# A PSUM bank for VectorE's small operands in a four-layer graph network

## What is computed

```
L0: (1 + eps) * x + segment_sum(relu(x[src] + edge48), dst)
L1: h = in_deg > 0 ? segment_sum(x[src] * ci[src], dst) * cj : x;   relu(h @ W.T + b)
L2: relu(segment_sum(norm * x[col], row) @ W.T + b)
L3: msg = (silu(edge40 @ W1.T + b1) @ W2.T + b2 + logit(type)) * x[dst] * cutoff * node_vec[dst]
    layernorm(x + segment_sum(msg, src) / segment_sum(node_vec[dst], src)) * gamma + beta
```

## Time and profile before

| | us |
|---|---|
| median of 3 runs (3310.13 to 3343.74) | 3333.56 |
| the profiled execution | 3348.9 |
| its span | 3347.1 |
| VectorE busy | 2025.7 (61%) |
| GpSimd busy | 1965.7 (59%) |
| TensorE busy | 774.6 (23%) |
| ScalarE busy | 640.9 (19%) |

### The profile page before, as it was taken

The page is one execution under the profiler, slowest core; times in us unless marked ns, Lnnn a source line. Parts: engine busy times, 40 slices in busy tenths (PEclk is TensorE's granted clock), DMA queues, the critical chain, the costliest instruction groups (busy, mean ns, idle before and its releaser), DMA issues.

```text
span 3347.1 us, 18878 instructions
## 1 busy us (share of the span) xinstructions
PE 774.6 (23%) x3478; PEld 547.8 (16%) x3478; DVE 2025.7 (61%) x2590; ACT 640.9 (19%) x1034; POOL 1965.7 (59%) x1768
## 2 busy tenths in 40 slices
PE   1182000000455653777832200000340000000000
PEld 0020000000355642444522200000340000000000
DVE  2187689768555554444543640788548968948551
ACT  0000102210222222333311100222111223221110
POOL 5703647770355456555247772777757777673776
PEclk7585555555565665555555555555555555555555
DMA  3105827660132232111000299344222212210000
GB/s 107 21 0 199 307 57 282 236 208 11 54 111 95 98 103 55 23 23 23 17 12 16 24 78 78 110 132 133 78 61 66 82 55 78 65 51 6 15 15 15
DMA packets 154317, 268.03 MB, mean 80 GB/s; under 512 B 87656, under 2 KB 112314, under 8 KB 154146
## 3 DMA queue, kind: packets, MB, share of 16 engines
q1 hardware_dynamic: 92786, 198.90, 21.4%
q0 software_dynamic: 56448, 44.04, 7.5%
q10 hardware_dynamic: 5040, 24.69, 2.0%
HBM read 135.62 MB, written 137.21 MB: 82 GB/s over the span
## 4 chain that ended last, share of the span: by engine, by line
issue 23%; POOL 21%; DVE 20%; PE 13%; another core or an unknown queue 9%; ACT 6%; DMA 4%; SPq 1%; DVEq 1%; ACTq 0%; POOLq 0%
POOL ring L425 10%; POOL out L463 6%; POOL x_table L463 5%; ACT sq L568 2%; DVE mu L1261 2%; DVE var L1270 2%; PE psT L845 2%; PE psO L860 2%; DVE du L1264 2%; PE psA L898 2%; PE psA L951 2%; DMA x_table<-sumb,put 1%; PE psG L956 1%; DVE sumb L1207 1%
## 5 line engine op out<-in xcount | busy, mean ns | idle before, releaser
L463 POOL DMA_INDIRECT y_table<-sumb,put x196 | 208.3, 1063 | 309.8 <-ACT sumb L595 252.2
L425 POOL DMA_INDIRECT ring<-in_xaux,srcI x196 | 189.1, 965 | 228.6 <-ACTq L562 141.5
L463 POOL DMA_INDIRECT x_table<-sumb,put x196 | 225.2, 1149 | 158.3 <-ACT sumb L595 91.6
L425 POOL DMA_INDIRECT ring<-edge_records,dstI x196 | 231.6, 1182 | 118.9 <-issue 61.0
L425 POOL DMA_INDIRECT ring<-y_table,srcI x196 | 203.9, 1040 | 159.2 <-ACTq L545 99.5
L425 POOL DMA_INDIRECT ring<-h_by_src,zd x196 | 235.3, 1200 | 89.0 <-issue 60.7
L425 POOL DMA_INDIRECT ring<-x_table,srcI x196 | 228.0, 1163 | 97.9 <-issue 57.9
L425 POOL DMA_INDIRECT ring<-xa_table,dstI x196 | 224.1, 1143 | 103.2 <-issue 64.8
L463 POOL DMA_INDIRECT out<-sumb,put x196 | 220.1, 1123 | 107.7 <-issue 60.8
L831 PE MATMUL psG<-ident,tail 128*49 128x128 f32 x10 | 4.5, 447 | 1137.1 <-DVEq L1013 1093.8
L1270 DVE TENSOR_REDUCE var<-sq 128x28 f32<-128x1344 f32 x119 | 181.2, 1552 | 142.1 <-ACT sq L568 137.1
(11 more groups left out here) (281 smaller groups left out, 3043.0 us busy)
## 6 DMA issues: line engine op xcount, KB each, us to landing
din<-in_xaux SPq DMA_DIRECT2D x56, 728.0 KB
x_table<-do SPq DMA_DIRECT2D x56, 672.0 KB
din<-x_table SPq DMA_DIRECT2D x56, 672.0 KB
xa_table<-din SPq DMA_DIRECT2D x28, 728.0 KB
y_table<-GX SPq DMA_DIRECT2D x28, 672.0 KB
out<-do SPq DMA_DIRECT2D x28, 672.0 KB
records_by_src<-ring ACTq DMA_DIRECT2D x14, 693.0 KB
GX<-records_by_src ACTq DMA_DIRECT2D x14, 693.0 KB
```

The source lines that it names most:

```text
L425: pool.indirect_dma_start(ring[:, h, t, 0:w], None, table, bass.IndirectOffsetOnAxis(ap=of[:, c * H + t:c * H + t + 1], axis=0), **skip).t ...
L463: pool.indirect_dma_start(table, bass.IndirectOffsetOnAxis(ap=put[:, c * H + t:c * H + t + 1], axis=0), stage[:, h, t, :], None, bounds_ch ...
```

## The change

One PSUM bank, `psS`, takes over the place of five small SBUF tiles: the row sums `mu` and the inverse deviations `srs` (28 columns for each of two blocks), the centred bias `rbc`, and copies of gamma (`gammaP`), beta (`betaP`), the carry (`carryP`) and of what `t0` holds at its last step (`t0P`). VectorE writes them there and reads them from there as one of the two tensors of an instruction; the large tensor of the instruction stays in SBUF. The rotating banks of the product go from six to five: `psO1` is gone, and the sixth, seventh and eighth group of a pair use the banks of the first three. The one product of the edge network that used `psO1` uses `psS`, at a time when it holds nothing that is read later.

```diff
-        mu = sb("mu", [P, 2, R])
-        srs = sb("srs", [P, 2, R])
-        rbc = sb("rbc", [P, D])
...
-        psO = [ps("psO0"), ps("psO1"), psA, psB, psC, psG]
+        psS = ps("psS")
+        psO = [ps("psO0"), psA, psB, psC, psG]
+        mu = psS[:, 0:2 * R].rearrange("p (h c) -> p h c", h=2)
+        srs = psS[:, 56:56 + 2 * R].rearrange("p (h c) -> p h c", h=2)
+        rbc, gammaP, betaP, carryP = (psS[:, 112 + k * D:112 + (k + 1) * D] for k in range(4))
+        t0P = psS[:, 304:304 + CE]
...
-                    elif k >= 6:
-                        pe.wait_ge(mm_used.sem, used - 4)
+                    elif k >= 5:
+                        pe.wait_ge(mm_used.sem, used - 3)
...
-                        last = T.matmul(psO[k % 6][:, j * 96:(j + 1) * 96], hT[0:97, g % 2, j * P:(j + 1) * P],
+                        last = T.matmul(psO[k % 5][:, j * 96:(j + 1) * 96], hT[0:97, g % 2, j * P:(j + 1) * P],
...
                 one(V.tensor_copy(carry[:, :], psG[:, P:P + D + 1]))
+                one(V.tensor_copy(carryP, carry[:, 0:D]))
...
-                one(V.tensor_tensor(su[:, :, :], along(mask[:, cols]), down(carry[:, 0:D]), ALU.mult))
+                one(V.tensor_tensor(su[:, :, :], along(mask[:, cols]), down(carryP), ALU.mult))
...
-            one(V.reciprocal(t0[:, :], t0[:, :]))
+            one(V.reciprocal(t0P, t0[:, :]))
...
-                one(V.tensor_tensor(su[:, :, :], M[:, cols, :], along(t0[:, cols]), ALU.mult))
+                one(V.tensor_tensor(su[:, :, :], M[:, cols, :], along(t0P[:, cols]), ALU.mult))
...
             counts(t0[:, :])
+            one(V.tensor_reduce(carry[:, 0:1], rows[:, 0, :], X, ALU.add))
+            one(V.scalar_tensor_tensor(rbc, carry[:, 0:1].broadcast_to([P, D]), -1.0 / D, rows[:, 0, :],
+                                       ALU.mult, ALU.add))
+            V.tensor_copy(gammaP, rows[:, 1, :]).then_inc(own.sem, own.add())
+            one(V.tensor_copy(betaP, rows[:, 2, :]))
             dve.sem_inc(S["by_src"], 1)
...
-                    V.tensor_tensor(DU[h], wide(h, D), down(rbc[:, :]), ALU.add).then_inc(S["centered"], 1)
+                    V.tensor_tensor(DU[h], wide(h, D), down(rbc), ALU.add).then_inc(S["centered"], 1)
...
-                    V.tensor_tensor(DO[h], along(sr2[:, h, :]), down(rows[:, 1, :]), ALU.mult
+                    V.tensor_tensor(DO[h], along(sr2[:, h, :]), down(gammaP), ALU.mult
...
-                    V.tensor_tensor(DU[h], DU[h], down(rows[:, 2, :]), ALU.add).then_inc(own.sem, own.add())
+                    V.tensor_tensor(DU[h], DU[h], down(betaP), ALU.add).then_inc(own.sem, own.add())
```

More of the change, by code:

```diff
@@ L939, in factors @@
                 for g in range(R // 4):
-                    bank = (psB, psC, psB, psC, psB, psC, psO[1])[g]
+                    bank = (psB, psC, psB, psC, psB, psC, psS)[g]
                     pe.wait_ge(ma.sem, ma.up())
@@ L1024, in _ @@
             one(V.tensor_scalar(rows[:, 0, :], rows[:, 0, :], 0.0, None, ALU.max))
-            one(V.tensor_reduce(mu[:, 0, 0:1], rows[:, 0, :], X, ALU.add))
-            one(V.scalar_tensor_tensor(rbc[:, :], mu[:, 0, 0:1].broadcast_to([P, D]), -1.0 / D, rows[:, 0, :],
-                                       ALU.mult, ALU.add))
             dve.sem_inc(S["init"], 1)
@@ L1319, in _ @@
                 norm([(0, su[:, :, :], su[:, :, :], XS[:, cols, :])])
-                one(V.tensor_tensor(M[:, cols, :], XS[:, cols, :], along(t0[:, cols]), ALU.mult))
+                one(V.tensor_tensor(M[:, cols, :], XS[:, cols, :], along(t0P[:, cols]), ALU.mult))
                 dve.sem_inc(S["rows_new"], 1)
@@ L1328, in taken @@
                     V.scalar_tensor_tensor(DU[h][:, 8 * g:8 * g + n, :],
-                                           psO[(4 * h + g) % 6][:, 0:n * D].rearrange("p (c d) -> p c d", d=D), 0.0,
+                                           psO[(4 * h + g) % 5][:, 0:n * D].rearrange("p (c d) -> p c d", d=D), 0.0,
                                            x(g, n), ALU.max, ALU.add).then_inc(mm_used.sem, mm_used.add())
@@ L1375, in factors @@
                     dve.wait_ge(mo.sem, mo.up())
-                    one(V.tensor_tensor(prod, (psB, psC, psB, psC, psB, psC, psO[1])[g][:, 0:4 * Z].rearrange(
+                    one(V.tensor_tensor(prod, (psB, psC, psB, psC, psB, psC, psS)[g][:, 0:4 * Z].rearrange(
                         "p (c z) -> p c z", z=Z), ohd[:, OH[g], :, :], ALU.mult))
@@ L1572, in _ @@
                 carried(cols)
-                one(V.tensor_tensor(su[:, :, :], M[:, cols, :], along(t0[:, cols]), ALU.mult))
+                one(V.tensor_tensor(su[:, :, :], M[:, cols, :], along(t0P[:, cols]), ALU.mult))
                 one(V.tensor_tensor(su[:, :, :], su[:, :, :], XS[:, cols, :], ALU.add))
                 norm([(0, su[:, :, :], su[:, :, :], su[:, :, :])])
-                one(V.tensor_tensor(su[:, :, :], su[:, :, :], down(rows[:, 1, :]), ALU.mult))
-                one(V.tensor_tensor(su[:, :, :], su[:, :, :], down(rows[:, 2, :]), ALU.add))
+                one(V.tensor_tensor(su[:, :, :], su[:, :, :], down(gammaP), ALU.mult))
+                one(V.tensor_tensor(su[:, :, :], su[:, :, :], down(betaP), ALU.add))
                 one(V.tensor_tensor(su[:, :, :], su[:, :, :], XS[:, cols, :], ALU.add))
```

## The result

The changed kernel took **3399.99 us** (median of 4 runs, 3390.99 to 3412.56) beside 3338.65 us of the kernel before: ratio 1.019, 95% interval 1.014 to 1.025. It is 61 us slower where 56 us less were forecast. The profiled execution has a span of 3402.3 us, 55.2 more than before.

A forecast was written before the change was run, and what follows sets the result against it. GpSimd's indirect DMAs, held up by VectorE instructions reading two SBUF tensors, were taken to bound most stages, with `y_table` a chain of other engines. Terms -20 - 5 - 15 - 4 - 14 + 1 + 1 = -56 us gave 3277 us, range 3250 to 3315.

The forecast's parts named there:

- the line on `y_table`: `y_table` stage, 869 to 1264 us: a chain of VectorE, TensorE and ScalarE; GpSimd's stalls go but nobody waited: 0.
- `xa_table`, -20 forecast: `xa_table` stage, bound by GpSimd: its stall over twelve turns falls from 35 to 15 us: -20 us (-16 to -24).
- `edge_records`, -15 forecast: `edge_records` loop: the bound passes to VectorE, which saves six ring waits of about 2.5 us each: -15 us.
- `x_table` gathered and `h_by_src`, -4: Gathers of `x_table` and `h_by_src`, 2361 to 3011 us: VectorE sets the pace, gains only at the ends: -4 us.
- `out`, -14: `out` loop at the program's end: every stall of GpSimd counts, 30.2 us falls to 15: -14 us (-9 to -20).
- `x_table` scatter, -5: `x_table` scatter: less GpSimd stall in its first seven turns, later savings lost waiting for stores: -5 us (-2 to -9).
- Banks, PSUM operands, copies, +2: Added costs: five banks in the dense product +1 us, PSUM operands of VectorE 0, four `carry` copies +1 us.
- Rival (c): Each norm's two short links: readers wait for small PSUM writes just made; at 0.5 us a link 3377 us; 6%.
- (B): Theory after the result: TensorE's signals come late while GpSimd issues indirect DMAs; GpSimd no longer held by VectorE worsens it.
- (C): Theory after the result: VectorE's own PSUM reads and writes disturb TensorE, at most together with GpSimd's issues.

The follow-up runs named there:

- free chip: Chip where VectorE gets 196 or 197 instructions done at 50 to 100 us beside GpSimd's DMAs; changed kernel against the kernel before: 0.982 to 0.983.
- second job: Changed kernel run once more as it is, against the kernel before, on another chip: ratio 0.982, 2901.6 us against 2955.4.
- paced kernel before: Kernel before with one short GpSimd memset, and a wait for it, ahead of each indirect DMA of the `y_table` and `x_table` scatters: 1.027 of the kernel before.
- third job's two kernels: Against the kernel before: the changed kernel, 0.983; and six banks with SBUF operands in the product loops, PSUM operands elsewhere, 0.987.
- coupled chips: Chips where VectorE gets only 18 to 20 instructions done at 50 to 100 us beside GpSimd's DMAs; changed kernel against the kernel before: 1.018 and 1.019.

## Why the prediction was wrong

**The failed step** is the line on `y_table`: "the stage is a chain between VectorE, TensorE and ScalarE. Stalls go, nobody waited for them. **0**." The chain is right and so is it that nobody waited for GpSimd. Missing is that on this chip the chain runs at a speed that depends on what GpSimd does. On the chip of the result the 0 was +24 us in the scatter and +34 in the gather behind it, in whose second turn the last pair of the product stands; the same omission made `x_table` +34 instead of -5 and the stretch from the first gather of `x_table` to the first of `h_by_src` (2414.9 to 2758.4 us, before 2361.0 to 2688.8), which holds the w2 product, +16 instead of about -2.

The trace of before had the sign. In the earlier trace rows TensorE and VectorE are each busy little more than half of the time and ScalarE a quarter; I read that as dependence alone. The two windows shown above, with VectorE at 5.93 of 50 us beside 41 issues and at 50 of 50 where GpSimd rests, lie in a stretch where the change has no term, and I read nothing there.

**The other terms.** A free chip shows them without the disturbance. No trace of the kernel before as it is was taken on one, so I set the changed kernel of the second job beside the paced kernel before; they differ in the two scatters in more than the change but not in the other tables:

- `xa_table`, -20 forecast: first to last start 283.3 us against 303.1, **-19.8**. On the chip of the result it was 299.1 against 324.0.
- `edge_records`, -15 forecast: start to the start of the next gather 284.4 against 292.7, **-8.3**. Six waits for the ring of 2.49 us went, as said, but each gave way to another:

```profile
2291.54 1.29 DVE L1493 TENSOR_TENSOR sub<-ring 128x672 f32<-128x672 f32 x1
2295.23 1.66 DVE L1206 TENSOR_TENSOR_SCAN sumb<-mask,sub 128x720 f32<-128x720 bf16 x1 [2.40 <-ACT mask L534]
2296.80 2.99 DVE L1462 TENSOR_TENSOR du<-din,psS 128x1344 f32<-128x1344 f32 x2
```

(Timeline of the changed kernel, the place of the earlier trace rows.) The scan waits 2.40 us for ScalarE's copy of the mask, where before it waited 0.85: that copy had been made while VectorE stood at the ring. Of 2.49 us 1.55 are handed on, and an iteration takes 41.7 us instead of 42.7. What was next late behind the ring I had not looked up.

- `x_table` gathered and `h_by_src`, -4: -1.6 us.
- `out`, -14: 267.7 us against 280.1, **-12.4**.
- `x_table` scatter, -5: 6.0 us between the third job's two kernels, which differ in the operands of these loops.
- Banks, PSUM operands, copies, +2: nothing against it in any run.

Together with 3 us in `y_table` that is some 51 us of 56. The total on free chips was -54, -49 and -53 us in three jobs. The mechanism was right for a chip on which GpSimd's issues leave the other engines alone. That the sum came so near there is in part luck: `edge_records` gave little more than half of its term, and `y_table`, priced at 0, gave 3 us. On the chip of the result the forecast gains came too, from start to start of the tables 26 us in `xa_table`, 5 in `edge_records`, 2 in `h_by_src` and 12 in `out`, 45 us together. Against them stand 24 us in the scatter to `y_table`, 36 from the gather of `y_table` to the next table, 18 from the scatter to `x_table` to the next (its 34 less the 16 of the shorter wait) and 16 in the stretch with the w2 product; and 8 us came ahead of the first loop that the change touches, a difference that no run explains. That makes the 55 us of the span. Rival (c) named the sign and about the size of the result (3377) for a reason that isn't there.

**What is shown and what isn't.** Shown: the loss sits in the product loops, goes with the small operands there and not with the bank, doesn't come from writing the rows, falls on pairs that have issues beside them, and was seen on both coupled chips that ran the changed kernel and on none of the three free ones. Only argued: that on such a chip it is GpSimd's freedom from VectorE (B) and not an effect that VectorE's PSUM accesses have only together with GpSimd's issues (C). For B: with no port contention left the `y_table` issues take 972 ns instead of 1063, and all 28 of a block stand in one pair; the changed kernel with pauses reached 0.999 on a coupled chip with every operand in PSUM, while the changed kernel stood at 1.018 and 1.019 in other jobs. But the pauses moved ScalarE's waits too. How much of the loss is rate and how much phase, why a chip is slow beside GpSimd, and whether the late thing is the signal or the supply of instructions, no run told.

## What to carry to other kernels

Freeing an engine may cost the others something: before pricing a lifted stall at zero or better, look for a stretch where the other engines work beside that engine and one where it rests, and compare their rates; here the first 250 us had both. When a wait goes, name the next one from the trace, because part of it is usually handed on (1.55 of 2.49 us here). And take a change of 2% to more than one chip: this one is 0.982 to 0.983 on three and 1.018 to 1.019 on two. SBUF operands in the loops with a product gave 0.989 with six banks and 0.991 with five on coupled chips, and 0.987 with six on a free one (five banks had no run there), so the version with six beats the kernel before on both kinds, by about 1%, where the change as made wins only on one.

## What the runs showed of the hardware

- The same kernel takes 2955 us on one chip and 3352 on another. The difference is in what other engines get done beside GpSimd's indirect DMAs: while VectorE and TensorE take turns, 19 VectorE instructions in 50 us with 41 issues, or 196 with 40.
- Without issues the coupled chip loses nothing: VectorE and TensorE are busy 50 of 50 us at 200 to 250 us.
- TensorE's granted clock differs with it: 0.50 (the 1.2 GHz level) at 50 to 100 us on the coupled chip, where TensorE is busy 8.34 of 50 us, and 1.00 (2.4 GHz) on the free one, where it is busy 48.64.
- A PSUM operand frees GpSimd whether it is the first or the second input, and costs VectorE nothing: 1550 ns against 1555 for 1344 elements with PSUM as the second input. The Trainium skill's page "VectorE: DVE Perf Modes", section "The TRN2 errata", has a fixed part of 120 cycles from PSUM and 58 from SBUF and so would add 62 cycles for it; the measurement decides against that here.
